# Two-layer gated cross-attention on one core: Silu taken from Tanh, FFN weights turned on VectorE, another order of steps and drain

## The reference

```python
q = rmsnorm(x_hat @ Wq.T); k = rmsnorm(ctx @ Wk.T); v = ctx @ Wv.T   # x_hat: x normalised over its features
x = x + tanh(g_xattn[l]) * (softmax(q @ k.T / sqrt(128) + mask) @ v @ Wo.T)
# layer 0 FFN, MX quantised in blocks of 32: weights to fp4, activations to fp6
h = silu(x6 @ w_gate4.T) * (x6 @ w_up4.T);  x = x + tanh(g_ffn[0]) * (fp6(h) @ w_down4.T)
# layer 1 FFN: one 512 x 512 int4 linear with permuted inputs and a bias
x = x + tanh(g_ffn[1]) * (x_hat @ w_int4.T + bias)
```

## Time and profile before

| | us |
|---|---|
| median of 3 launches | 1395.19 (1393.07 to 1395.94) |
| the profiled launch | 1396.21 |
| its span in the profile | 1393.9 |
| TensorE matmul busy | 1349.6 (97%) |
| VectorE, ScalarE, GpSimd busy | 960.2 (69%), 839.8 (60%), 659.4 (47%) |

### The profile page before, as it was taken

One profiled execution on the slowest core, in us unless ns is written; L12 is line 12 of the kernel. 1 busy time (PEld: TensorE's weight loads), 2 busy tenths in 40 slices (PEclk: granted clock), 3 DMA queues, 4 the chain that ended last, 5 costly groups with the idle time before them and its releaser, 6 DMA issues.

```text
span 1393.9 us, 25793 instructions
## 1 busy us (share of the span) xinstructions
PE 1349.6 (97%) x7908; PEld 1138.3 (82%) x7924; DVE 960.2 (69%) x1949; ACT 839.8 (60%) x3271; POOL 659.4 (47%) x686
## 2 busy tenths in 40 slices
PE   5899999999999999999999999999999999999997
PEld 4788888888888888767677688888888888888886
DVE  4678788787878788577767766766555565565665
ACT  3666666666666666556666555655666666565541
POOL 2536656565747666346666533532433333332232
PEclk9999999999999999999999999999999999999999
DMA  8011021111121110010200011201010010100001
GB/s 280 1 46 54 20 70 41 62 53 58 53 64 47 49 63 26 1 46 1 77 31 1 1 31 47 77 31 54 31 46 30 3 68 5 45 30 1 1 16 45
DMA packets 33707, 59.46 MB, mean 43 GB/s; under 512 B 2784, under 2 KB 25952, under 8 KB 29536
## 3 DMA queue, kind: packets, MB, share of 16 engines
q1 hardware_dynamic: 33632, 58.54, 12.7%
HBM read 56.43 MB, written 2.10 MB: 42 GB/s over the span
## 4 chain that ended last, share of the span: by engine, by line
PE 75%; issue 10%; POOL 6%; DVE 5%; ACT 3%; DMA 1%; SPq 0%; POOLq 0%; DVEq 0%; ACTq 0%
PE bank L1050 52%; PE bank L1042 7%; PE bank L1130 7%; PE bank L1179 5%; PE bank L1187 1%; POOL rstd L510 1%; POOL f_iq L536 1%; PE bank L1170 1%; DVE amax L822 1%; DVE f_q L829 1%; DVE f_s L846 1%; ACT probs L622 1%; POOL probs L549 1%; ACT L616 1%; ACT f_s L616 1%
## 5 line engine op out<-in xcount | busy, mean ns | idle before, releaser
L472 POOL TENSOR_TENSOR w_lo<-w_raw,w_hi (+1 forms) x150 | 227.5, 1533 | 198.6 <-ACT w_hi L635 197.9
L667 ACT ACTIVATE squares<-bank 128x128 bf16<-128x128 f32 x512 | 134.7, 278 | 255.1 <-PE bank L1050 255.1
L951 DVE SCALAR_TENSOR_TENSOR probs<-bank,mask_sb 128x512 f32<-128x512 f32 x128 | 88.2, 689 | 229.4 <-PE bank L1130 229.4
L622 ACT ACTIVATE probs<-probs,negmax 128x128 f32<-128x128 f32 x512 | 198.7, 391 | 8.3 <-DVE negmax L955 8.0
L506 POOL TENSOR_TENSOR meansq<-sumsq,scalars 128x5 f32<-128x5 f32 x128 | 28.3, 221 | 321.3 <-ACT squares L667 321.3
L510 POOL TENSOR_TENSOR rstd<-meansq,scalars 128x5 f32<-128x5 f32 x128 | 152.6, 1193 | 10.9 <-POOL meansq L506 1.3
L1050 PE MATMUL bank<-w_hi,oT_hi 128*128 (+1 forms) x512 | 150.6, 416 | 0.0
L1050 PE MATMUL bank<-w_hi,xT_hi 128*128 (+1 forms) x512 | 143.7, 403 | 0.6 <-DVE w_lo L770 0.6
L1050 PE MATMUL bank<-w_lo,xT_hi 128*128 (+1 forms) x512 | 138.4, 392 | 0.0
L1050 PE MATMUL bank<-w_lo,oT_hi 128*128 (+1 forms) x512 | 138.2, 391 | 0.0
L1050 PE MATMUL bank<-w_hi,xT_lo 128*128 (+1 forms) x512 | 137.6, 391 | 0.0
(11 more groups left out here) (133 smaller groups left out, 3065.5 us busy)
## 6 DMA issues: line engine op xcount, KB each, us to landing
w_raw<-in_wq SPq DMA_DIRECT2D x16, 1024.0 KB, 5.0
w_raw<-in_wo SPq DMA_DIRECT2D x16, 1024.0 KB, 4.8
fw_raw<-in_ffn_w SPq DMA_DIRECT2D x36, 192.0 KB, 2.3
w_raw<-in_wk SPq DMA_DIRECT2D x16, 256.0 KB, 5.5
w_raw<-in_wv SPq DMA_DIRECT2D x16, 256.0 KB, 5.5
x_sb<-in_x SPq DMA_DIRECT2D x4, 512.0 KB, 9.9
ctx_raw<-in_ctxT SPq DMA_DIRECT2D x4, 512.0 KB, 10.5
out<-x_sb SPq DMA_DIRECT2D x8, 256.0 KB, 2.0
```

The costliest lines, as they stand in the source:

```text
L472: last = nc.gpsimd.tensor_tensor(lo, raw, hi.bitcast(FP32), ALU.subtract)
L622: last = nc.scalar.activation(probs[:, h * P:(h + 1) * P], probs[:, h * P:(h + 1) * P], ACT.Exp, bias=negmax[:, h:h + 1], accum_out=rowsum ...
L667: last = nc.scalar.activation(squares[:, h // 2, (b + 1) % 4, h % 2, :], psQ[:, h * P:(h + 1) * P], ACT.Square, scale=SCALE, accum_out=sum ...
L951: nc.vector.scalar_tensor_tensor(heads(probs[:, :]), heads(psSQ[:, :]), SCALE, mask_sb[:, :].unsqueeze(1).to_broadcast([P, REP, P]), ALU.m ...
```

## The change

- **Silu.** ScalarE takes Tanh of g/2 out of psA into `f_s` (`gate_tanh`); VectorE forms (1+tanh)·g from `f_s` and psA, then multiplies psB by it in place, and quantises from psB. `gate_up` signals its two halves apart; the gate half waits for `up_used`, the up half for `six_read` (the six-bit values of the chunk before are read).
- **Layer 0's FFN weights.** The host lays them out so that 32x32 transposes suffice. VectorE turns each piece (`piece_turned`, after rinv, one step after its rounding); TensorE's transposes go; ScalarE copies from SBUF instead of PSUM.
- **Order.** In QUANT steps and in those with `t.down` or `t.next`, VectorE's order becomes masked scores, qn, pT_lo, negmax (`qn_first`). In FFN steps chunk 2 comes after the Q projection, the hidden transposes after the output projection, x's add after `hidden(0)`, GpSimd's scalings and ScalarE's exponentials (after qT where `t.down` or `t.next`) move as well.
- **Drain.** Steps from 128 on have lists of their own on VectorE and ScalarE (`drain`). TensorE transposes a tile after the output projection and P.V, that of the last tile inside the product of the one before; the last product, its add and its store are done in halves of 256 columns. ScalarE's `drain` does oT_hi, pT_hi, the exponentials, xT_hi, in that order.

The diff, cut to its core (the same blocks at their old places, renamed semaphores and blank lines are left out):

```diff
                     step(i + b, b, PLAIN, i // BATCHES)
-            for s in range(LAST0, END):
+            for s in range(LAST0, END if drain is None else ALL):
                 step(s, s % BATCHES, LAST, None)
+            for s in range(ALL, END if drain is not None else ALL):
+                drain(s)
@@ -346,6 +352,10 @@
             return q * QSTEPS + b
+        def qn_first(kind, t):
+            return kind == QUANT or t.down is not None or t.next is not None
...
-            for b in range(BATCHES):
+            for b in range(BATCHES - 1):
...
                 sp.dma_start(out_v[b], x_sb[:, b, :]).then_inc(stored, 16)
-            sp.wait_ge(stored, 16 * BATCHES)
+            for k, cols in enumerate(LAST_HALVES):
+                sp.wait_ge(h_acc, BATCHES + k)
+                sp.dma_start(out_v[BATCHES - 1][:, cols], x_sb[:, BATCHES - 1, cols]).then_inc(stored, 16)
+            sp.wait_ge(stored, 16 * (BATCHES + 1))
...
-                if t.down is not None:
-                    scale_six(1, t.down)
...
+                if t.down is not None:
+                    scale_six(1, t.down)
...
                     ln_rstd_of(NORM["ffn", t.norm])
+                if t.down is not None:
+                    scale_six(2, t.down)
+                if t.norm is not None:
                     if t.down is not None:
-                        pool.wait_ge(clipped, SIX[2, t.down] + 1)
+                        pool.wait_ge(up_used, len(CHUNKS) * (t.down + 1))
...
                     normalise(NORM["next", t.acc], t.acc, qn[:, :])
+                if t.gate is not None:
+                    scale_six(0, t.gate)
...
                     round_piece(q, b)
-                if t.gate is not None:
-                    scale_six(0, t.gate)
...
+            def gate_tanh(c, i):
...
                 width = CHUNKS[c][1]
-                act.wait_ge(clipped, SIX["in" if c == 0 else c - 1, i] + 1)
-                act.wait_ge(gu_ps, n + 1)
-                nc.scalar.activation(f_s[:, 0:width], psA[:, 0:width], ACT.Silu, scale=1 / FP6_UNIT).then_inc(silu_done, 1)
+                if c == 0:
+                    act.wait_ge(clipped, SIX["in", i] + 1)
+                wait(act, up_used, n)
+                act.wait_ge(gate_ps, n + 1)
+                nc.scalar.activation(f_s[:, 0:width], psA[:, 0:width], ACT.Tanh, scale=0.5 / FP6_UNIT).then_inc(tanh_done, 1)
...
                     nc.scalar.activation(pT_hi[:, :], psPO[:, :], ACT.Copy).then_inc(pt_hid, 1)
+                if q is not None and 0 < b <= QSTEPS:
+                    piece, width = quant_piece(q, b - 1), PIECE_BLOCKS[b - 1] * P
+                    first = (q * GROUP_BLOCKS + PIECE_AT[b - 1]) * P
+                    act.wait_ge(wt_turned, piece + 2)
+                    nc.scalar.activation(wT[:, bass.ds(first, width)], fw_turned[:, 0:width], ACT.Copy).then_inc(wt_sb, 1)
...
+                    xT_upper(2 * BATCHES + t.last)
+                if t.gate is not None:
+                    gate_tanh(0, t.gate)
+                if has(n, 0):
+                    act.wait_ge(rs_done, n + 1)
+                    act.wait_ge(v_lod, n + 1)
+                    wait(act, kt_ps, n)
+                    nc.scalar.activation(kn[:, :], psKV[:, 0:P], ACT.Copy, scale=rstd[:, REP:REP + 1]).then_inc(kn_done, 1)
+                if has(n, 1) and t.next is None and t.down is None:
+                    softmax_exp(n)
+                if t.next is not None:
@@ -713,8 +728,10 @@
                     nc.scalar.activation(qT[:, :], psSQ[:, :], ACT.Copy).then_inc(qT_sb, 1)
+                if has(n, 1) and (t.next is not None or t.down is not None):
+                    softmax_exp(n)
                 if t.gate is not None:
-                    silu(1, t.gate)
+                    gate_tanh(1, t.gate)
@@ -811,6 +845,14 @@
+            def piece_turned(q, b):
+                width, piece = PIECE_BLOCKS[b] * P, quant_piece(q, b)
+                dve.wait_ge(fw_quantised, piece + 2)
+                dve.wait_ge(wt_sb, piece + 1)
+                nc.vector.transpose(fw_turned[:, 0:width], fw_out[:, 0:width]).then_inc(wt_turned, 1)
...
-                link(nc.vector.scalar_tensor_tensor(blocks_of(q8), blocks_of(src), 2.0 ** -5, each(v, BLOCK),
-                                                    ALU.mult, ALU.mult, saturate=False))
+                nc.vector.scalar_tensor_tensor(blocks_of(q8), blocks_of(src), 2.0 ** -5, each(v, BLOCK),
+                                               ALU.mult, ALU.mult, saturate=False).then_inc(six_read, 1)
+                dve.wait_ge(six_read, k + 1)
@@ -840,13 +883,24 @@
             def hidden(c, i):
...
                 width = CHUNKS[c][1]
-                dve.wait_ge(silu_done, n + 1)
-                nc.vector.scalar_tensor_tensor(f_s[:, 0:width], psB[:, 0:width], 1 / FP6_UNIT, f_s[:, 0:width],
+                dve.wait_ge(tanh_done, n + 1)
+                nc.vector.scalar_tensor_tensor(f_s[:, 0:width], f_s[:, 0:width], 1.0, psA[:, 0:width],
+                                               ALU.add, ALU.mult).then_inc(gated, 1)
+                dve.wait_ge(gated, n + 1)
+                dve.wait_ge(gu_ps, n + 1)
+                nc.vector.scalar_tensor_tensor(psB[:, 0:width], psB[:, 0:width], 0.5 / FP6_UNIT ** 2, f_s[:, 0:width],
...
                 dve.wait_ge(up_used, n + 1)
-                quantise6(f_s[:, 0:width], c, i)
+                quantise6(psB[:, 0:width], c, i)
+            def maximum(n):
+                dve.wait_ge(masked, n)
+                nc.vector.tensor_reduce(negmax[:, :], heads(probs[:, :]), AX.X, ALU.max,
+                                        negate=True).then_inc(nm_done, 1)
...
                     nc.vector.reciprocal(rinv[:, :], rowsum[:, :]).then_inc(rinv_done, 1)
+                if q is not None and 0 < b <= QSTEPS:
+                    piece_turned(q, b - 1)
@@ -942,6 +996,8 @@
                     moments(NORM["ffn", t.norm], t.norm)
+                if t.down is not None:
+                    hidden(2, t.down)
...
                         mask_sb[:, :].unsqueeze(1).to_broadcast([P, REP, P]), ALU.mult, ALU.add).then_inc(masked, 1)
-                    dve.wait_ge(masked, n)
-                    nc.vector.tensor_reduce(negmax[:, :], heads(probs[:, :]), AX.X, ALU.max,
-                                            negate=True).then_inc(nm_done, 1)
+                if has(n, 1) and not qn_first(kind, t):
+                    maximum(n)
@@ -964,7 +1019,11 @@
                                             ALU.mult).then_inc(qn_done, 1)
-                if has(n, 2) and t.gate is None:
+                if has(n, 2) and qn_first(kind, t):
+                    probs_lower(n)
+                if has(n, 1) and qn_first(kind, t):
+                    maximum(n)
+                if has(n, 2) and t.gate is None and not qn_first(kind, t):
@@ -979,6 +1038,8 @@
                                             ALU.mult).then_inc(kT_sb, 1)
+                if t.gate is not None:
+                    hidden(0, t.gate)
@@ -988,7 +1049,6 @@
                 if t.gate is not None:
-                    hidden(0, t.gate)
...
+            def drain(n):
+                t = Tiles(n, LAST)
...
+                if has(n, 3):
+                    dve.wait_ge(o_hid, n - 2)
+                    nc.vector.tensor_tensor(oT_lo[:, :], psPO[:, :], oT_hi[:, :].bitcast(FP32),
+                                            ALU.subtract).then_inc(o_lod, 1)
+                if t.last is not None:
+                    dve.wait_ge(x_acc, LAST0 + t.last + 1)
+                    moments(NORM["last", t.last], t.last)
+                if has(n, 2):
+                    dve.wait_ge(pt_hid, n - 1)
+                    nc.vector.tensor_tensor(pT_lo[:, :], psPO[:, :], pT_hi[:, :].bitcast(FP32),
+                                            ALU.subtract).then_inc(pt_lod, 1)
+                if ALL < n and Tiles(n - 1, LAST).last is not None:
+                    xT_lower(2 * BATCHES + Tiles(n - 1, LAST).last)
+                if has(n, 1):
+                    dve.wait_ge(s_ps, n)
+                    dve.wait_ge(pt_ps, n - 1)
+                    nc.vector.scalar_tensor_tensor(
+                        heads(probs[:, :]), heads(psSQ[:, :]), SCALE,
+                        mask_sb[:, :].unsqueeze(1).to_broadcast([P, REP, P]), ALU.mult, ALU.add).then_inc(masked, 1)
+                    dve.wait_ge(masked, n)
+                    nc.vector.tensor_reduce(negmax[:, :], heads(probs[:, :]), AX.X, ALU.max,
+                                            negate=True).then_inc(nm_done, 1)
+                if t.last is not None:
+                    dve.wait_ge(xT_ps, 2 * BATCHES + t.last)
+                    normalise(NORM["last", t.last], t.last, f_s[:, :])
+                if has(n, 3):
+                    dve.wait_ge(y_ps, n - 2)
+                    dve.wait_ge(x_acc, n - 3)
+                    xb = x_sb[:, batch_of(n, 3, None), :]
```

(69 more changed lines are left out.)

129 lines of the change are left out of this document (65 added, 64 removed).

## The result

| | before | after |
|---|---|---|
| median, us | 1394.99 (4 runs, 1393.07 to 1395.94) | 1380.38 (4 runs, 1378.14 to 1380.47) |
| the profiled launch, its span | 1396.21, 1393.9 | 1378.14, 1376.3 |

The ratio is 0.9893 [0.9876, 0.991]: 1.1% faster, where 0.9% slower was forecast. The time lies inside the range given, the sign is wrong.

What follows compares the result with a forecast made beforehand. TensorE was taken as busy throughout the quantising loop, but partly waiting in the FFN and drain. Terms +28 + 0 - 9 - 5.5 = +13.5 on 1396.2, less 1.0 for the median, gave 1408 us; range 1376 to 1432.

Steps and rivals of the forecast that it cites:

- the ring is bare: Rival, chance 0.2: less collision in the quantising loop and little in the FFN, -14 us, ending at 1380.
- the sixth group: Eight ZONE steps behind the QUANT groups, keeping the old order: -1.3 us against some late kT, taken as 0.
- Part 3: QUANT steps, negmax after qn and pT_lo: TensorE stalls at the next K/V projection, +28 us (+6.6 to +60).
- the ring: Quantising-loop cycle negmax, exponentials, qT, oT_hi, masked scores, negmax: 10.83 us with two splits, 9.88 with one, against TensorE's 9.53.
- rstd: GpSimd's rstd in the quantising loop, done about 0.35 us after qn could start, in four steps a group.
- Rival (c): Quantising loop: GpSimd's rstd blocks VectorE's piece, +45 us at most, 1440, or from 1418 if half; chance 0.18.
- Part 2: VectorE's transposes of the weight pieces fill a hole before oT_lo: cost nothing, otherwise 0.5 us a step.
- Part 1: TensorE's weight transposes go: 1.3 us a group, 7.7 in all, as far as nothing else sets the step.
- Part 4: FFN steps: 2.3 us of waiting a tile goes, less 0.7 and 0.4: -9 us (about -15 to about 0).
- the clip: FFN: VectorE's clip could meet GpSimd's normalise, shifting later work by about 1.2 us, some 0.7 seen by TensorE.
- the psA transposes: FFN: transposes of the next layer's tile into psA wait for chunk 2's product, about 0.4 us late.
- Part 5: Drain: transposes after the output projection and a halved last add remove TensorE idle time, -5.5 us (-4 to -6.5).

Runs made afterwards that it cites:

- pe_turns: Changed kernel, but TensorE transposes the quantised weights again and VectorE doesn't; qn and pT_lo stay ahead of negmax in the loop: 1381.30 us.
- max_first: Changed kernel, but in the weight-quantising loop negmax stands again straight behind the masked scores: 1370.02 us.
- amax_psum: On max_first, the quantiser's block maxima and their inverses live in PSUM bank psA instead of SBUF: 1364.47 us.
- silu_new_order: Changed kernel with Silu in place of Tanh in the FFN, so table loads return and the output differs from the reference: 1388.34 us.
- old_drain: Changed kernel with the old drain: last normalised tiles transposed at their old place, last projection and stores whole: 1385.75 us.

## Why the prediction was wrong

**The sum.** +28 in the loop, 0, -9 and -5.5 stood against +8.4, +0.1, -17.7 and about -5.4. Both misses went the same way, and together they turned the sign. The rival *the ring is bare* has the time (1380) and a chance of 0.2, but hit it in part by luck: its reason, no collision of the pieces with GpSimd in the loop, did not come true (L835 takes 1.20 in the two-split step), and its +6.6, -15, -6 and -1.3 for the sixth group are off by +1.8, -2.7, +0.6 and +1.4, which nearly cancel. No rival had a shorter ring with the collision in it.

**Part 3, the ring: right as a mechanism, mis-sized by 20 us. This is the step that failed most.** Its rows are all there, two-split and one-split steps in turn, late exponentials, negmax after negmax at 10.49. It was 10.83 in the sum. The 0.34 between are 0.16 from qT to oT_hi, which start 0.48 apart when neither waits, where 0.64 was taken from rows that did not follow at once; 0.10 for the exponentials, whose end was taken for the start of what follows, though rows overlap by a tenth; the rest in hundredths. For the one-split step 9.48 came for 9.88, and the opening step took 9.76, not 10.0. Over a group (opening step, three of each kind, closing step) that is 0.2 + 1.2 + 1.0 + 0.1, 2.5 of the 3.9 us between 83.1 and 79.2. The other 1.4 was rstd: four times 0.35, which did not occur. A ring within 0.3 us of another engine's own time is an excess that changes by its own size with such errors: for the one-split step the whole predicted excess of 0.35 was the error.

**Rival (c), rstd blocks VectorE: refuted.** VectorE's L844 and L846 took their usual 0.35 and 0.36 while rstd ran (480.73 to 482.29 above). It was rstd that grew, from 1.17 to 1.56, where it started 0.10 behind VectorE's pass L838 (480.64 to 481.20, two inputs in SBUF); in the one-split step it started 0.23 behind L841 and took 1.17. The Trainium skill, "SBUF — State Buffer", on the shared port pair, would have the later one wait for a whole instruction. For GpSimd's w_lo the trace and the experiments agree with it: L835 at 1.20 ends with GpSimd's second w_lo, the product with rinv, with two SBUF inputs, runs once the first w_lo is through, and the pass with operands in PSUM is free. For VectorE's passes that start behind rstd, 5 elements a partition, they do not agree.

**Part 2, the turn: right** (0.58, in the hole before oT_lo; pe_turns shortened the long step by at most 0.1). With negmax first the hole is shorter: the turn waits 0.39 for `fw_out` and ends late enough that the product with rinv starts 0.11 behind w_lo and is locked, the pass over the maxima behind it too, and steps are 9.83.

**Part 1: right as a bound, and mostly not collected.** The changed kernel has none of the 7.7 in the loop, max_first 2.1 with all six groups, amax_psum nearly all (381.52 for 387.50 in the loop, 76.21 for 77.61 in the sixth group, 7.4). The prediction said "as far as nothing else sets the step"; for the sixth group its 0 was right (+0.1).

**Part 4, the FFN: mis-sized by 9 us, and its reason was in part wrong.** The -17.7 lies outside its own bounds (0 to -15). The 2.3 us of waiting a tile did go, 2.27 of it (29.91 to 27.64). The terms that failed are the two deducted from it, 0.7 and 0.4, together the 9 us: the clip met GpSimd's `normalise` and was not held (0.43 long at 649.81, in the middle of a normalise from 648.99 to 651.07), and the psA transposes waited 0.2, not 0.4. And the tables, which the part put first as what stood between gate_up(0) and gate_up(1), gave nothing by themselves. The Trainium skill, "ScalarE: Activation LUTs", that Exp and Tanh share a set, holds here (no load is left in the FFN's rows); what the loads cost depended on the order: 0 us for sixteen, 8 us for 32. Rows that hint at it were in the trace of before and were not read: in the FFN ScalarE waits 39.4 us for VectorE's clip and 16.4 for the K/V projection. What made the gain is the form and the four queues' order together; with Silu and its 32 loads back, they still keep 10.0 of the 17.7 (silu_new_order, 306.23). Each part tried alone was slower or nothing: loads gone 0.0, form +5.4, the third chunk moved +5.1, form and that move +33.9. How the rest of the order (x's add behind `hidden(0)`, GpSimd's scalings, ScalarE's exponentials) shares the gain was not tried piece by piece and stays open.

**Part 5: right**, 5.4 by old_drain for 5.5.

**The sixth group, and the chances.** The order there was kept and no ring appeared, as said: behind the loop its first step took 10.01, the others 9.50 to 9.75. The error of judgment was in how the terms were joined: 0.45 on a sum in which a ring of ten terms and three collisions that the trace did not show (rstd, the clip, the psA transposes) were all taken at the costly side, and 0.28 in all on anything faster than no change.

**A version that beats both** is amax_psum: negmax first in the loop, the block maxima and inverses in PSUM, all else as changed. 1364.47 us, 2.3% under the kernel before, with TensorE at its own time through the loop.
